# Layer-0 projections: weights loaded whole and split in place, K and V first, six tiles turned ahead

## The reference

```python
xn = _layernorm(x, axis=-1)
q = ((x @ Wq[l].T + bq[l]) * scaling).reshape(n, H, DH)   # in _L0_gnn_ref, x = xn for l = 0
k = (x @ Wk[l].T).reshape(n, H, DH)
v = (x @ Wv[l].T).reshape(n, H, DH)
```

## Time and profile before

| what | value |
|---|---|
| median of three runs | 3077.7 us |
| span of the profiled execution | 3095.6 us |
| PE busy | 2657.9 us, 86% |
| DVE busy | 1629.2 us, 53% |
| ACT busy | 1321.1 us, 43% |
| POOL busy | 1115.8 us, 36% |

### The profile page before, as it was taken

One profiled execution on the slowest core, in us unless ns is written; L12 is line 12 of the kernel. 1 busy time (PEld: TensorE's weight loads), 2 busy tenths in 40 slices (PEclk: granted clock), 3 DMA queues, 4 the chain that ended last, 5 costly groups with the idle time before them and its releaser, 6 DMA issues.

```text
span 3095.6 us, 78344 instructions
## 1 busy us (share of the span) xinstructions
PE 2657.9 (86%) x32605; PEld 2143.5 (69%) x32605; DVE 1629.2 (53%) x3272; ACT 1321.1 (43%) x3690; POOL 1115.8 (36%) x1130
## 2 busy tenths in 40 slices
PE   5999997999999999758899788888888678599998
PEld 4877885777777777546488577777777465477777
DVE  5236785555555555456512355555554645656553
ACT  3324443555555555422232255555555322333432
POOL 0000002666666666400001267777777111222110
PEclk8999998999999999979999899999999889799998
DMA  5642003988899998641024489999999431122211
GB/s 195 228 175 107 31 28 140 317 313 316 309 331 322 317 325 297 222 121 41 14 97 154 160 321 354 352 349 347 350 347 352 126 113 57 38 89 92 69 59 58
DMA packets 231795, 621.75 MB, mean 201 GB/s; under 512 B 39008, under 2 KB 45792, under 8 KB 231427
## 3 DMA queue, kind: packets, MB, share of 16 engines
q0 software_dynamic: 137088, 466.78, 42.2%
q1 hardware_dynamic: 94339, 149.78, 14.6%
HBM read 538.80 MB, written 103.39 MB: 207 GB/s over the span
## 4 chain that ended last, share of the span: by engine, by line
PE 60%; DMA 16%; DVE 8%; POOL 7%; issue 6%; ACT 2%; SPq 0%; DVEq 0%; POOLq 0%; ACTq 0%
PE ps L1179 6%; DMA Y<-KVd,srcE 5%; PE ps L574 5%; PE ps L575 4%; PE ps L576 4%; DMA aggd<-stage,segs 4%; PE ps L1222 4%; PE ps L1209 4%; PE ps L774 3%; POOL Y L1096 3%; PE ps L942 2%; PE ps L944 2%; PE ps L943 2%; PE ps L1186 2%; PE ps L1872 2%
## 5 line engine op out<-in xcount | busy, mean ns | idle before, releaser
L1096 POOL DMA_INDIRECT Y<-KVd,srcE x449 | 430.2, 958 | 230.6 <-issue 115.8
L1370 ACT ACTIVATE stage<-ps,stage 128x128 f32<-128x128 f32 x832 | 294.8, 366 | 115.3 <-PE ps L1186 112.4
L1096 POOL DMA_INDIRECT WA<-KVd,srcE x186 | 179.3, 964 | 361.8 <-PE ps L576 268.1
L1351 ACT ACTIVATE work<-ps 128x512 f32<-128x512 f32 x309 | 179.8, 597 | 303.8 <-PE ps L1179 303.5
L1179 PE MATMUL ps<-ident,Y 128*128 128x128 f32 x1796 | 252.2, 280 | 32.2 <-DMA Y<-KVd,srcE 26.8
L1351 ACT ACTIVATE G<-ps 128x512 f32<-128x512 f32 x315 | 181.8, 597 | 223.5 <-PE ps L1179 223.1
L1277 DVE COPY G<-ps 128x512 f32<-128x512 f32 x208 | 143.8, 691 | 245.8 <-PE ps L1186 243.0
L574 PE MATMUL ps<-Wh,xs 128*128 128x512 f32 x600 | 238.7, 398 | 31.2 <-DVE xs L514 31.2
L1179 PEld LDWEIGHTS ps<-ident,Y 128*128 128x128 f32 x1796 | 199.2, 143 | 70.5 <-issue 49.3
L575 PE MATMUL ps<-Wl,xs 128*128 128x512 f32 x600 | 236.9, 395 | 0.0
L576 PE MATMUL ps<-Wh,xs 128*128 128x512 f32 x600 | 236.5, 394 | 0.0
(11 more groups left out here) (383 smaller groups left out, 6775.2 us busy)
## 6 DMA issues: line engine op xcount, KB each, us to landing
KVd<-stage SPq DMA_DIRECT2D x96, 256.0 KB, 2.0
aggd<-work SPq DMA_DIRECT2D x6, 2048.0 KB, 7.4
Qd<-stage SPq DMA_DIRECT2D x48, 256.0 KB, 2.0
G<-aggd SPq DMA_DIRECT2D x48, 256.0 KB, 2.7
Y<-KVd,srcE POOLq DMA_INDIRECT x449
Y<-in_x SPq DMA_DIRECT2D x4, 1536.0 KB, 14.7
G<-mixq SPq DMA_DIRECT2D x24, 256.0 KB
mixd<-rowsb SPq DMA_DIRECT2D x24, 256.0 KB
```

Of the source, the lines that this page charges most:

```text
L1096: pool.indirect_dma_start(out=kvs[a], out_offset=None, in_=KVd[l][:, :], in_offset=bass.IndirectOffsetOnAxis(ap=srcE[:, n:n + 1], axis=0)) ...
L1351: act.activation(kT[n % len(kT)], banks(l)[place_of(l, "k", n) % len(banks(l))][:, :], ACT.Copy).then_inc(out_a, 1)
L1370: last = act.activation(pT[g % len(pT)][:, P * i:P * (i + 1)], SC[g % 2][:, P * i:P * (i + 1)], ACT.Exp, bias=smin[:, t:t + 1], scale=-1.0 ...
```

## The change

A new tensor `Wraw0`, of the size of three whole weights, lies in the place of `Wl0`. Each weight is loaded with one transfer of 1024 KB into it; ScalarE writes the high parts from there to `Wh0`, and VectorE writes the low part over the raw one. No load waits for a buffer. SyncE issues x and weights in the order group 0, K, group 1, V, group 2, group 3, Q.

Ahead of the loop stand group 0 alone (`HEAD = 6`) and the splitting of the eight quarters of K and V; ScalarE's order there is the root, K's quarters, two tiles, V's quarters, four tiles. In the loop `head_pe(u)` turns tile u + 5, from step 1 on; `head_dve` normalises group 1 behind step 1's low part, group 2 behind step 4's, group 3 behind step 10's, group 4 behind step 15's; the four quarters of Q are split in steps 4 to 8, one a step. The edge tables still begin at step 12 (`INDEX_AT`). The scaling of Q's bias stands behind the low parts of the first 26 steps, in both layers. TensorE waits for K's four quarters before K, for V's before V, and for Q's before step 25.

```diff
+        with ExitStack() as under:
+            Wraw0 = under.enter_context(nc.sbuf_tensor("Wraw0", [P, 3, 4, 512], F32))
         Wl0 = tensor("Wl0", [P, 3, 4, 512], F32R)
...
+            six_tiles(0)
+            raw_weights(1)
+            six_tiles(1)
+            raw_weights(2)
+            six_tiles(2)
+            six_tiles(3)
+            raw_weights(0)
             sp.wait_ge(filled, 3)
...
-            for n in range(12):
-                w, k = n // 4, n % 4
-                if n >= 4:
-                    sp.wait_ge(w_lo, n - 3)
-                sp.dma_start(stage[:, k, :], A[("WqT", "WkT", "WvT")[w]][0, k * P:(k + 1) * P, :]).then_inc(w_in[k], 16)
...
+        CUTS = [(w, k) for w in (1, 2, 0) for k in range(4)]
+
+        def low_weight(n):
+            w, k = CUTS[n]
+            dve.wait_ge(w_hi, n + 1)
+            dve.tensor_tensor(Wl0[:, w, k, :], Wraw0[:, w, k, :], Wh0[:, w, k, :].bitcast(F32), ALU.subtract
+                              ).then_inc(w_lo, 1)
...
+        def high_weight(n):
+            w, k = CUTS[n]
+            act.wait_ge(w_in[w], 16)
+            act.activation(Wh0[:, w, k, :], Wraw0[:, w, k, :], ACT.Copy).then_inc(w_hi, 1)
...
-        HEAD = 12
+        HEAD, LATER, INDEX_AT = 6, 5, 12
...
-            if u + HEAD < NT:
-                columns_pe(u + HEAD)
+            if u and u + LATER < NT:
+                columns_pe(u + LATER)
...
-            if u in (1, 5, 11):
-                norm_x_dve({1: 2, 5: 3, 11: 4}[u])
-            if u >= HEAD:
+            if u in (1, 4, 10, 15):
+                norm_x_dve({1: 1, 4: 2, 10: 3, 15: 4}[u])
+            if u in (5, 6, 7, 8):
+                low_weight(u + 3)
+            if u >= INDEX_AT:
                 next(index_of_dve, None)
...
-            dve.wait_ge(row_in, ROW_Q[l])
-            dve.tensor_scalar(rowsb[:, 0, :], rowsb[:, 0, :], 0.125, None, ALU.mult).then_inc(*step_v.up())
-
...
             for u in range(NT + 1):
                 low(u)
                 beside(u)
+            dve.wait_ge(row_in, ROW_Q[l])
+            dve.tensor_scalar(rowsb[:, 0, :], rowsb[:, 0, :], 0.125, None, ALU.mult).then_inc(*step_v.up())
...
+        spread_act(0)
+        for n in range(4):
+            high_weight(n)
+        for t in range(2):
+            columns_act(t)
+        for n in range(4, 8):
+            high_weight(n)
+        for t in range(2, HEAD):
+            columns_act(t)
```

More of the change, by code:

```diff
@@ L217, in first_loads, with six_tiles @@
         def first_loads():
-            for g in range(4):
+            def six_tiles(g):
                 sp.dma_start(Yt0[:, 6 * g:6 * g + 6, :],
@@ L221, in first_loads, with raw_weights @@
                              ).then_inc(x_in[g], 16)
+            def raw_weights(w):
+                sp.dma_start(Wraw0[:, w], kpo(A[("WqT", "WkT", "WvT")[w]][0])).then_inc(w_in[w], 16)
+            six_tiles(0)
[5 more added lines that the diff above has]
+            raw_weights(0)
             sp.wait_ge(filled, 3)
@@ L477, in head_act @@
         def head_act(u):
-            if u in (0, 4, 10):
-                spread_act({0: 2, 4: 3, 10: 4}[u])
+            if u in (0, 3, 9, 14):
+                spread_act({0: 1, 3: 2, 9: 3, 14: 4}[u])
+            if u in (4, 5, 6, 7):
+                high_weight(u + 4)
         def tail_act(u):
-            if u + HEAD < NT:
-                columns_act(u + HEAD)
+            if u and u + LATER < NT:
+                columns_act(u + LATER)
             if u >= NT + 2 and u % 2:
@@ L560, in qkv_pe @@
         def qkv_pe(l, xs, Wh, Wl, beside):
-            pe.wait_ge(w_lo, (12, 40)[l])
             for u in range(2 * NT):
                 r = ROWS[u % NT]
+                if l == 1 and u == 0:
+                    pe.wait_ge(w_lo, 40)
+                if l == 0 and u == NT:
+                    pe.wait_ge(w_lo, 12)
                 pe.wait_ge(x_lo, TURN0[l] + u + 1)
@@ L571, in qkv_pe @@
                         pe.wait_ge(kv_out, 2 * NT * l + f + 1)
+                    if l == 0 and u == 0:
+                        pe.wait_ge(w_lo, 4 * w)
                     for k in range(4):
@@ L614, in build @@
             columns_pe(t)
-        for g in range(2):
-            norm_x_dve(g)
-        low_weights()
+        norm_x_dve(0)
+        for n in range(8):
+            low_weight(n)
         index_of_pe, index_of_act, index_of_dve = index_pe(), index_act(), index_dve()
@@ L2063, in cut_act @@
             if n < 12:
-                act.wait_ge(w_in[n // 4], 64)
+                act.wait_ge(w_in[n // 4], 32)
                 act.activation(Wh1[:, n // 4, n % 4, :], Wraw[:, n // 4, n % 4, :], ACT.Copy).then_inc(w_hi, 1)
```

## The result

The changed kernel takes 3065.0 us (median of seven runs, 3059.5 to 3074.2) beside 3083.7 us for the kernel before (median of seven, 3074.9 to 3098.2). The ratio is 0.9944 with a 95% interval of 0.9927 to 0.9962: 17.3 us less, between 11.7 and 22.5. Two later comparisons of the same pair of kernels gave 0.9959 (0.9943 to 0.9976) and 0.9953 (0.9935 to 0.9971), 12.6 and 14.5 us. The forecast was 14.9 us less and a time of 3062.8. One caution about the time itself: with more runs the kernel before turned out 6 us slower than the median from which the forecast started, so the gain, not the time, is what the forecast is to be held against. That 3065.0 lies only 2.2 us from 3062.8 is in part luck: the median that the sum started from was 6.0 us too low, and the first comparison shows 2.4 us more gain than the forecast.

A forecast was written before the change was run, and what follows sets the result against it. TensorE waits for its first product until 42.17 us, then is itself the bound. First product 17.7 us earlier, turned tiles 2.8 later: 14.9 us off the 3077.7 median gives 3062.8 us, range 3055 to 3071.

The forecast's parts named there:

- The first product: Head of the kernel: TensorE's first product at 24.5 us instead of 42.17, 17.7 us earlier, most of it transfer.
- The turned tiles: K and V tile loop: six tiles now turned between products, 0.47 us each, 2.8 us later, with no cover.
- What costs nothing: Tile loop and queues: moved normalisations, Q splits, bias scaling and later SyncE issues stay hidden; VectorE's slack is 1.65 us.
- The rival that ended slower: Tile loop: VectorE's normalisation groups come too late and stop TensorE; groups twice as long give 18 us, 3081; chance 0.02.
- The bias scaling: Head: scaling Q's bias, 0.34 us in the chain, moves behind the 26 low halves, 5 us ahead of its use.
- The clock: Behind the first product: same loss at TensorE's lower clock as before; no loss or twice it, 2.6 us either way.
- Loads landing out of order: Head loads: sharing engines, V lands at 29.2 us, first product 35.8, gain 3.6, time up to 3074; chance 0.05.
- eight large pieces: Head loads, out-of-order rival: V lands with the last of these, at 29.2 us instead of 17.8.
- The gain given back later: Behind the phase: a transfer or queue ends unmoved by the head; half lost gives 3070, all 3077.7; chance 0.06.
- The sign that all later stages move "by the same": Behind the head: the 499 us transfer some 15 us earlier, and all later stages moved by the same.
- the median it started from: Whole kernel: 3077.7 us before the change, some 18 below the profiled span; the 14.9 us are taken from it.

The follow-up runs named there:

- the experiment: The changed kernel with the scaling of Q's bias put back ahead of the first low half; ratio to the kernel before 0.999 (0.997 to 1.001).
- second and third trace: The changed kernel traced twice more with no edit; ratios to the kernel before 0.9959 (0.9943 to 0.9976) and 0.9953 (0.9935 to 0.9971).

## Why the prediction was right

**The first product.** Forecast 24.5 us, measured 24.10. The order of the links was right, and each came within half a microsecond: V landed at 17.4 (17.8 forecast), its splits ended at 19.6 (20.0), the last eviction at about 22.8 (23.2). The one size that was off is the load: a group of x was taken as 4.27 us; moving V behind two of them moved its landing by 25.48 - 17.39 = 8.09 us, 4.05 each. That "most of these 24.5 us are transfer" holds for this order of ScalarE's queue alone: with K's product asking for K alone, the same loads let it start at 18.80.

**The turned tiles.** 0.47 us each: 5.91 against 5.44 in both kernels. TensorE stops four times in the Q part. The products behind the first and the last stop, in its timeline before:

```profile
197.81 0.50 PE L574 MATMUL ps<-Wh,xs 128*128 128x512 f32 x1 [1.85 <-DVE xs L514]
...
223.30 0.50 PE L574 MATMUL ps<-Wh,xs 128*128 128x512 f32 x1 [1.85 <-DVE xs L514]
```

And after:

```profile
182.64 0.55 PE L592 MATMUL ps<-Wh,xs 128*128 128x512 f32 x1 [1.85 <-DVE xs L525]
...
209.77 0.50 PE L592 MATMUL ps<-Wh,xs 128*128 128x512 f32 x1 [1.85 <-DVE xs L525]
```

The first is 15.2 us earlier, which is 18.07 - 2.8 less 0.1 for the lower level at the start. At 499 us 13.5 are left. The 1.7 us are lost between these rows: from the first to the last of them it takes 25.49 us before and 27.13 after. The stops are the same four of up to 1.9 us (7.4 in all, as in the earlier trace rows), but what follows them is not: behind some of them the matmuls take 0.43 us for 4 to 5 us, the lower level, and the next stop then comes 9.6 us after the last and not 8.0. This happened behind two of the four stops in both traces of the kernel before, behind three in the first two traces of the changed kernel, and behind two in its third, where the stretch takes 25.47 us and the long transfer starts 2.9 us earlier than in the first. That the lower level would return there as often as before was an assumption the prediction did not state; whether the changed kernel makes a third stay at the lower level likelier, three traces do not tell.

**What costs nothing.** The cover on VectorE came out as read. Group 2, now behind step 4, ends where its low half says, in VectorE's timeline:

```profile
50.83 2.83 DVE L280 TENSOR_SCALAR Y<-Y,mv,rs 128x512 f32<-128x512 f32 x6
53.58 0.68 DVE L525 TENSOR_TENSOR xs<-xT,xs 128x512 fp32r<-128x512 f32 x1
```

The low half ends at 54.26, and TensorE wants it 0.44 us behind 55.48, at 55.92: a slack of 1.66 us, 1.65 forecast. The rival that ended slower needed these groups to be late; none was. On SyncE's queue the last load ahead of the stores was issued at 28.60 (29.7 forecast) and the first store at 30.27 (30.1), when ScalarE had evicted it; the queue was free 1.2 us before, at 28.60 + 0.43 = 29.03, so no load held it:

```profile
28.60 0.43 SPq L246 DMA_DIRECT2D rowsb<-in_gbq x1
30.27 3.01 SPq L609 DMA_DIRECT2D KVd<-stage x2
```

**What was mis-sized.** The bias scaling. The prediction gave it 0.34 us in the chain and counted it among what costs nothing, which is true of its new place. It did not ask what the old place would have cost in the new kernel: the row is issued behind 3 MB more, and the experiment has VectorE standing 12.35 us for it. The sum did not suffer, since the change moves it, but a reader of the prediction might have left that line out as a trifle and lost ten of the 14 us.

**The clock.** Taken as unchanged, with 2.6 us either way. In the profiled run it was unchanged (5.4 us of the lower level, so 2.7 lost); in the second and third trace it was 6.3 and 2.9 us, and with the first product on K alone there was no lower level at all. All lie within the bounds of no loss and twice the loss. With the stays at the lower level in the Q part, which the prediction did not count, this is the main spread of the head from run to run.

**The rivals.** Loads landing out of order: refuted by V's landing at 17.4 us in the changed kernel, ahead of the groups of x issued behind it, and by V issued ahead of the second group of x, which landed 3.7 us earlier for 0.55 us of earlier issue. (The "eight large pieces" of this rival are seven, as in its sum.) The sentence of the Trainium skill that the prediction weighed (page "DMA: Bandwidth & Descriptors", section "Queues, rings and completion order") allows another order, and no run here showed one for loads of this size from one queue. The gain given back later: 13.5 of 15.2 us still stand at 499 us (13.7 on the mean of all traces), and the ratios give 12.6 to 17.3. The sign that all later stages move "by the same" was not met as it stands: at the first product of the second layer the traces are 20.5 us apart, and their spread behind it hides the rest. The weak part of the sum's frame was the median it started from, three runs and 6 us too low, told with the result.

## What to carry to other kernels

Where a queue of loads holds the start, price every instruction that waits for a load by where the load would land in the new order, also those that look like trifles. Read the limits in series: here the loads and the tiles prepared ahead each gave little alone, and the third limit, an engine's own queue, stood within 2 us of the second. The next step is then to ask what the first product needs, and to put nothing else ahead of it on any engine.

## What the runs showed of the hardware

SyncE's four large loads of the earlier trace rows were issued some 0.55 us apart until the fourth, which took 4.67 us to issue; in the changed kernel V's, again the fourth, stands 3.49 us in SyncE's timeline:

```profile
2.37 3.49 SPq L226 DMA_DIRECT2D Wraw<-in_WvT x1
```

In these traces three loads of 1 to 1.5 MB go into the queue at once, and the fourth holds SyncE for 3.5 to 4.7 us; an order of issue is thus also a limit on how early a small load behind large ones can start. The bias row, put back ahead of the first low half, shows it: it was issued at 28.54 us and landed at 32.96.

The level of TensorE's clock behind the same instructions was not the same from run to run: 5.4, 6.3 and 2.9 us of the lower level behind the first product in three runs of one kernel, at 24.10, 24.12 and 23.95 us, and the lower level again behind two or three of the four stops of 1.85 us in the Q part. The one is worth up to (6.3 - 2.9) / 2 = 1.7 us, the other 1.6, so a gain or loss under some 3 us up to the end of the projections cannot be laid to an edit from one trace.
